# Two-layer perceiver kernel: the running maximum closed one tile earlier, and its scaling, the mask's bias and the decays rearranged on ScalarE

## The chip, the cores and the metric

The kernel runs on one core of one Trainium2 chip. The metric is the device time in microseconds (us) of one execution. The engines are TensorE (PE in the profile; its weight loads are PEld), VectorE (DVE), ScalarE (ACT), GpSimd (POOL) and SyncE (SP), whose queue issues the DMA transfers. Each engine works through its own instructions in order and waits on semaphores for the others.

## The reference, cut to what matters

128 latent rows of 256 numbers attend, in two layers, over the same context of 12,544 rows. Between the two attentions and behind the second lie small linear-attention, feed-forward and convolution blocks; the change does not touch their arithmetic.

```python
def _layer0_attention(q_in, ctx, mask, Wq, bq, Wk, bk, Wv, bv):    # 16 heads of 16
    q, k, v = split(q_in @ Wq.T + bq), split(ctx @ Wk.T + bk), split(ctx @ Wv.T + bv)
    scores = einsum('bhqd,bhkd->bhqk', q * 16 ** -0.5, k)
    scores = scores + ((1.0 - mask) * -10000.0)[:, None, :, :]     # first layer only
    probs = softmax(scores, axis=-1)
    return einsum('bhqk,bhkd->bhqd', probs, v)
...
x = x + _layer0_attention(layernorm(x), ctx, mask, ...)
x = x + linear_attention_block(layernorm(x)); x = x + ternary_ffn(layernorm(x))
x = x + _layer1_attention(layernorm(x), ctx, ctx, ...)             # no mask
x = x + rwkv_block(layernorm(x)); x = x + ternary_conv_ffn(layernorm(x))
```

The feed-forward weights are rounded to three values before use ("ternary").

## The kernel before, in words

The 12,544 context rows are 98 tiles of 128. Eight tiles are a group, so a layer has 13 groups: 12 full ones and one of two tiles. Groups are numbered through both layers: 0 to 12 are the first layer's (`m < NG`), 13 to 25 the second's. Tiles within a group are 0 to 7, so the "sixth tile" is number 5.

The softmax is computed online. For each group the kernel needs the running maximum of the scores per query and head before the group's scores are made. These maxima come from cheap bf16 products of queries and keys (`product`, L1396 on TensorE), 32 per full group, which VectorE reads one by one from PSUM (`maximum`, L989 with the mask added in the first layer, L992 in the second), into `tile_max`. The products and readings for the next group, and the first ones for the group after it, are spread over the tiles of the present group by `count_at`: four products in an ordinary tile. When the 32 are read, `chain` closes the group on VectorE: a reduction of `tile_max` (L1009), in the first layer a scaling and a shift (L1012), then a maximum with the group before (L1017), with a wait between each. It runs in tile 6 (`CHAIN_AT`). In tile 7 (`ROWS_AT`) TensorE turns the result (`turn_max`, L1490), ScalarE copies it out as `max_rows` (`rows_out`, L714) and GpSimd subtracts the rows of the group before (`max_change`, L586). In tile 0 of the next group ScalarE makes the decay factors by three exponentials (`decay_out`, L707: one of 128x256, two of 64x256) and VectorE multiplies the accumulated sums in PSUM by them (`decay_sums`, L1040), before TensorE may add that group's first sums (`weigh`, L1471).

One tile of the first layer goes as follows. TensorE makes the scores of 16 heads (L1446 subtracts the maximum, L1450 multiplies). VectorE adds the mask to half of them (`bias_first`, L1057). ScalarE copies the other half out (`copy_second`, L724), and GpSimd adds the mask there (`add_bias`, L580). ScalarE then takes the exponential of the first half (L732), copies a projection out (`keys_out` L691 in even tiles, `values_out` L699 in odd ones), and takes the exponential of the second half. TensorE meanwhile weighs the values of the tile before (L1471) and projects keys (L1389) or values (L1374) of groups to come. In the second layer there is no mask: ScalarE takes the exponential straight from PSUM (`exp_scores`, L738).

The mask of the next group is turned into a bias by two VectorE instructions of 128x512, in tiles 4 and 5 (`mask_bias`, L1066). In tile 2 of group 3 VectorE also adds a bias to x and scales a bias of the second layer (L1139, L1141, `BIAS_AT`). GpSimd rounds three feed-forward weights (`ternary`, L560, L562, L564) in 72 pieces, one in every tile of groups 1 to 9; `TERN_AT` says where.

From tile 2 of a layer's last full group on, the tiles are "lone" (`lone`, `LONE_FROM`): there are no more maxima, and in the first layer VectorE adds the mask to both halves (`bias_last`, L1075). In the first layer's lone tiles `weigh` also writes a small matmul into the `ps_proj` bank between its two halves, for which it first waits until the bank's last reader is through (`proj_free`). The two-tile group's maximum is closed in tile 2 and its rows are copied out in tile 7. GpSimd makes that last group's mask bias itself (`bias`, L548), in tile 4 of the group before. Behind the 72 pieces the SP queue loads the weights of the middle blocks (L508, L424), because they overwrite the place of the unrounded ones.

In the second layer, groups 13 and 14 are split into two halves with a maximum of their own each (`is_split`, `stage`).

Of the kernel before, what the change touches and what calls it, by code (L numbers as in the profile page):

```python
# [5 lines left out]
ALU = mybir.AluOpType  # L6
# [32 lines left out]
def perceiver(nc, a, out):  # L39

    with ExitStack() as ctx:
# [28 lines left out]
        tile_max = sb("tile_max", [P, H, 2])  # L70
        block_max = sb("block_max", [P, H])
# [75 lines left out]
        TERN_AT = tuple(range(GT))  # L147
# [11 lines left out]
        def run_max(m):  # L159
            return max_of_head[m % 2][:, :]  # L160
# [62 lines left out]
        def chained(m, t):  # L223
# [46 lines left out]
        CHAIN_AT, ROWS_AT = 6, 7  # L270
        FIRST_AHEAD = 2

        def count_at(m, t):
# [9 lines left out]
            elif m == 0:  # L283
                now = (2, 2, 2) if 0 < t < 3 else (2, 0, 2) if t < CHAIN_AT else (2, 0, 0) if t == CHAIN_AT else now
            elif n + 1 < NG and size(m + 1) < GT:
                now = ((2, 0, 2), (2, 0, 2), (2, 0, 0))[t] if t < 3 else now
            elif n + 1 < NG and t <= CHAIN_AT:
                now = (2, 0, 2 if t < CHAIN_AT else 0)
            if n + 2 < NG and m != NG:
                ahead = (0, 0, 2) if t == CHAIN_AT else (2, 0, 2) if t > CHAIN_AT else ahead  # L290
# [60 lines left out]
        BIAS_AT = 3  # L351
# [170 lines left out]
        def _(pool):  # L522
# [73 lines left out]
            for m in range(BLOCKS):  # L596
# [3 lines left out]
                for t in range(size(m)):  # L600
# [4 lines left out]
                    if 0 < m <= 9 and t in TERN_AT:  # L605
                        ternary(GT * (m - 1) + TERN_AT.index(t))
# [4 lines left out]
                    if rowed(m, t):  # L611
                        max_change(rowed(m, t))
                    if TAPS_AT <= m < TAPS_AT + FC // 2 and t in (1, 3, 5):
# [32 lines left out]
        def _(act):  # L646
# [55 lines left out]
            def decay_out(s):  # L702
                act.wait_ge(sig("max_changes"), decays(s))
                need("acc_decayed", decays(s) - 1)
                for to, of, cols in ((slice(0, P), slice(0, P), slice(0, D)), (slice(0, 64), slice(64, P), slice(D, 2 * D)),
                                     (slice(64, P), slice(0, 64), slice(D, 2 * D))):
# [33 lines left out]
            def lent_out(m, t):  # L740
                if decayed_in(m, t):
                    decay_out(stage(m, t))
                if rowed(m, t):
                    rows_out(rowed(m, t), turn_bank(m, t))

# [11 lines left out]
            for l in range(2):  # L757
# [14 lines left out]
                if l == 0:  # L772
# [7 lines left out]
                    for u in range(4, len(FIRST) - 1):  # L780
                        first_out(u)
                        if u in (7, 8):
                            abs_sum(u - 7)
# [1050 lines left out]
```

## Time and profile before

| What | us |
|---|---|
| Median of 3 runs (1011.79 to 1016.0) | 1012.31 |
| The profiled execution, its own time | 1009.68 |
| Span of that execution in the trace | 1008.0 |
| TensorE busy | 938.2 (93%) |
| VectorE busy | 737.4 (73%) |
| ScalarE busy | 684.1 (68%) |
| GpSimd busy | 407.5 (40%) |

Shares are over the whole span. The first layer's attention runs from about 40 to 484 us, the middle blocks to about 540, the second layer's attention to about 966, and the last blocks to the end. The profiled execution lies 2.6 us below the median; its span leaves out 1.7 us around it. A busy interval of a matmul in the trace is longer than the time that it holds the array, so intervals overlap and TensorE's idle time looks smaller than it is: the distance from a tile to the same point of the next one says more.

### The profile page before, as it was taken

What the parts mean: (1) busy time and instruction counts of PE and PEld (TensorE: products, weight loads), DVE (VectorE), ACT (ScalarE), POOL (GpSimd) and SP (SyncE); (2) the same over time, 40 slices, a digit from 0 to 9 for tenths busy, and PEclk for the clock granted to TensorE, in tenths of its full rate; (3) what the DMA queues carried; (4) which work ended last, traced back from release to release, by engine and by line L of the source; (5) the groups of instructions that cost most, each with busy time, mean ns of one, the idle gap of its engine ahead of it and who ended that gap; (6) DMA issues with size and microseconds to landing.
All of it is one profiled execution on the core that took longest, in us unless ns stands there. A gap on an engine that the chain in (4) does not pass through costs nothing.

```text
span 1008.0 us, 37248 instructions
## 1 busy us (share of the span) xinstructions
PE 938.2 (93%) x16290; PEld 575.7 (57%) x16291; DVE 737.4 (73%) x1594; ACT 684.1 (68%) x953; POOL 407.5 (40%) x365
## 2 busy tenths in 40 slices
PE   8899999999999999997887789999999999999877
PEld 3355555555555655555563455656656666566666
DVE  5798999999999899885447766556555666556566
ACT  2678878888887888876563456566666666665753
POOL 4258988899889988750100010011101001110010
PEclk9999999999999999999999899999999999999999
DMA  8402201211220210123005001011001101000000
GB/s 336 146 21 84 86 24 64 86 36 53 86 84 5 86 55 8 65 96 125 1 12 198 1 2 45 2 44 45 20 26 45 44 3 44 13 3 3 3 1 6
DMA packets 14994, 53.08 MB, mean 53 GB/s; under 512 B 4336, under 2 KB 5744, under 8 KB 10992
## 3 DMA queue, kind: packets, MB, share of 16 engines
q1 hardware_dynamic: 14832, 50.70, 14.4%
q8 instruction: 129, 2.11, 0.9%
q14 instruction: 33, 0.27, 0.1%
HBM read 50.56 MB, written 0.13 MB: 50 GB/s over the span
## 4 chain that ended last, share of the span: by engine, by line
PE 64%; DVE 16%; issue 12%; ACT 6%; DMA 1%; SPq 0%; DVEq 0%; ACTq 0%; POOLq 0%
PE ps_proj L1374 14%; PE ps_out L1471 13%; PE ps_scores L1450 11%; PE ps_proj L1389 8%; PE ps_max L1396 7%; DVE unread L989 4%; PE ps_scores L1446 3%; DVE tile_max L992 2%; ACT probs L738 2%; ACT decay L707 2%; DVE probs L1057 1%; DVE probs L1075 1%; DVE masks L1066 1%; DVE tile_max L989 1%; DVE ps_out L1040 1%
## 5 line engine op out<-in xcount | busy, mean ns | idle before, releaser
L992 DVE TENSOR_REDUCE tile_max<-ps_max 128x1 f32<-128x512 f32 (+1 forms) x293 | 188.3, 674 | 124.6 <-PE ps_max L1396 122.0
L580 POOL TENSOR_TENSOR probs<-probs,masks 128x512 f32<-128x512 f32 x180 | 227.5, 1286 | 69.4 <-ACT probs L724 68.8
L732 ACT ACTIVATE probs<-probs 128x1024 f32<-128x1024 f32 x196 | 207.0, 1056 | 71.6 <-DVE probs L1057 56.4
L738 ACT ACTIVATE probs<-ps_scores 128x1024 f32<-128x1024 f32 x192 | 186.3, 1021 | 86.2 <-PE ps_scores L1450 86.1
L1450 PE MATMUL ps_scores<-q_pad,k_full 32*128 32x256 f32 x3072 | 236.0, 376 | 0.0
L1471 PE MATMUL ps_out<-probs,values 128*32 128x128 f32 x6272 | 216.6, 277 | 4.8 <-DVE ps_out L1040 2.8
L989 DVE CUSTOM_DVE_ANT_0 unread<-ps_max,masks 128x512 bf16<-128x512 f32 (+1 forms) x293 | 189.8, 674 | 34.9 <-PE ps_max L1396 33.4
L1450 PEld LDWEIGHTS ps_scores<-q_pad,k_full 32*128 32x128 f32 x3072 | 189.1, 186 | 8.5
L1471 PEld LDWEIGHTS ps_out<-probs,values 128*32 128x32 f32 x6272 | 159.2, 110 | 57.6 <-issue 51.4
L1396 PE MATMUL ps_max<-k_high,q_high 32*128 32x512 bf16 (+1 forms) x590 | 155.9, 382 | 32.4 <-DVE tile_max L992 15.4
L1374 PE MATMUL ps_proj<-wv,ctx_t 128*32 128x256 f32 x2752 | 164.9, 380 | 0.0
L1389 PE MATMUL ps_proj<-ctx_t,wk 128*32 128x512 f32 (+1 forms) x1360 | 159.3, 586 | 1.0 <-DVE tile_max L989 0.8
L571 POOL CAST k_high<-k_full 128x1024 bf16<-128x1024 f32 (+1 forms) x51 | 50.3, 990 | 218.5 <-ACT k_full L691 141.7
L1396 PEld LDWEIGHTS ps_max<-k_high,q_high 32*128 32x128 bf16 x590 | 37.7, 91 | 173.8 <-issue 68.9
L586 POOL TENSOR_TENSOR max_step<-max_rows 128x512 f32<-128x512 bf16 x26 | 30.6, 1177 | 259.7 <-ACT max_rows L714 259.7
L1446 PE MATMUL ps_scores<-max_rows,minus 32*128 32x512 bf16 x768 | 110.2, 382 | 7.7 <-ACT max_rows L714 4.1
L1374 PEld LDWEIGHTS ps_proj<-wv,ctx_t 128*32 128x32 f32 x2752 | 82.3, 110 | 48.6 <-issue 0.5
L1057 DVE TENSOR_TENSOR probs<-ps_scores,masks 128x1024 f32<-128x1024 f32 x90 | 109.7, 1219 | 0.0
L724 ACT COPY probs<-ps_scores 128x512 f32<-128x512 f32 x180 | 95.6, 584 | 0.9 <-PE ps_scores L1450 0.9
L699 ACT COPY values<-ps_proj 128x512 f32<-128x512 f32 x86 | 50.0, 582 | 47.6 <-PE ps_proj L1374 47.1
L691 ACT ACTIVATE k_full<-ps_proj,bk 128x512 f32<-128x512 f32 (+1 forms) x85 | 56.8, 669 | 29.7 <-PE ps_proj L1389 29.4
L1396 PE MATMUL ps_proj<-k_high,q_high 32*128 32x512 bf16 (+1 forms) x182 | 67.8, 372 | 2.1 <-ACT k_full L691 2.1
(302 smaller groups left out, 858.7 us busy)
## 6 DMA issues: line engine op xcount, KB each, us to landing
ctx_t<-in_ctx_t SPq DMA_DIRECT2D x23, 1024.0 KB, 5.9
masks<-in_mask_n SPq DMA_DIRECT2D x12, 512.0 KB, 3.6
masks<-in_mask_t SPq DMA_DIRECT2D x12, 512.0 KB, 4.0
room_w<-in_L_attn_f_w SPq DMA_DIRECT2D x2, 1024.0 KB, 9.0
room_w<-in_L_ffn_w SPq DMA_DIRECT2D x2, 1024.0 KB, 7.4
ctx_t<-in_ctx_t SPq DMA_DIRECT2D x2, 512.0 KB, 6.5
room_w<-in_L_ffn_w_gate SPq DMA_DIRECT2D x1, 1024.0 KB, 11.4
room_w<-in_L_ffn_w_up SPq DMA_DIRECT2D x1, 1024.0 KB, 13.8
```

The costliest lines, as they stand in the source:

```text
L580: nc.gpsimd.tensor_tensor(p, p, three(mask_t[m % 2], GT)[:, t, :].unsqueeze(1).to_broadcast([P, 4, P]), ALU.add).then_inc(sig("bias_added" ...
L732: nc.scalar.activation(prob(T, half), prob(T, half), ACT.Exp).then_inc(sig(f"exp_done{half}"), 1)
L738: nc.scalar.activation(prob(T, half), scores_in(m, t, half).rearrange("p a n -> p (a n)"), ACT.Exp).then_inc(sig(f"exp_done{half}"), 1)
L989: ins = v.tensor_tensor_reduce(unread[:, j % 2, 0:width(m)], max_bank(m, j)[:, 0:width(m)], mask_n[m % 2][:, half_cols(m, half)], 1.0, -3e ...
L992: ins = v.tensor_reduce(tile_max[:, h, half:half + 1], max_bank(m, j)[:, 0:width(m)], AX_X, ALU.max)
L1057: v.tensor_tensor(prob(T, 0).rearrange("p (h q) -> p h q", h=8), ps_scores[:, 0:2, :].rearrange("p a (h q) -> p (a h) q", q=P), three(mask ...
L1374: last = mm(bank[32 * g:32 * (g + 1), D * (t - at.start):D * (t - at.start + 1)], ctx_t[m % 3][:, t, c, keys], wv[l][:, c, :], start=(c == ...
L1389: last = mm(bank[32 * g:32 * (g + 1), 0:width(m)], wk[l][:, c, dims], ctx_t[m % 3][:, 4 * half:min(4 * half + 4, size(m)), c, :], start=(c ...
L1396: mm(bank[:, 0:width(m)], q_high[rows, c, zz, :], k_high[m % 2][rows, c, half_cols(m, half)], start=True, stop=True).then_inc(sig("max_rea ...
L1446: mm(banks[g], minus16[rows, :], max_rows[stage(m, t) % 2][rows, :], start=True, stop=True)
L1450: last = mm(banks[g][:, D * c:D * (c + 1)], k_full[m % 3][rows, c, P * t:P * (t + 1)], q_pad[rows, c, :], start=False, stop=True, skip_gro ...
L1471: last = mm(ps_out[VW * g:VW * (g + 1), P * c:P * (c + 1)], values[m % 2][:, t, h, :], prob(T, half)[:, P * o:P * (o + 1)], start=(t == 0 ...
```

## The change

1. The first layer's full groups close the next group's maximum in tile 5 in place of 6, and copy its rows out in tile 6 in place of 7 (`chain_at`, `rows_at`); `count_at` moves the readings to fit: of the 32 maxima of a group, the first ten (before: six) are now read right behind the closing of the group ahead of it. Group 0 gets six maxima in its tiles 3 and 4. The two-tile group is closed in tile 1 (first layer) or 2 (second), and in both layers its rows are copied out in tile 3.
2. `tile_max` has four columns, the running maximum being column 0 or 3 by turns, so that one reduction gives the new running maximum. Scaling, shift and conversion to bf16 become one ScalarE instruction on 128x16 (`max_out`), in both layers (a plain copy in the second), for which `turn_max` waits.
3. The mask's bias of groups 1 to 11 goes from VectorE to ScalarE (`mask_bias`), ahead of the first exponential of tiles 4 and 5.
4. The decays: in the first layer's full groups the 128x256 one is made in tile 7 and the other two in tile 0. They stand ahead of the tile's exponentials, in the second layer too, where all three stay in the first tile of a stage.
5. GpSimd's ternary pieces go to tiles 1, 2, 4, 5 and 7 of groups 1 to 10, five in group 0, and 17 in tiles 2 and 3 of group 11, behind that tile's `max_change`. The addition and scaling of `BIAS_AT` go from group 3, tile 2, to group 11, tile 4.

```diff
-        TERN_AT = tuple(range(GT))
+        TERN_AT = [(0, t) for t in range(3, 8)] + [(m, t) for m in range(1, 11) for t in (1, 2, 4, 5, 7)] + [(11, 2)] * 9 + [(11, 3)] * 8
...
-            return max_of_head[m % 2][:, :]
+            return tile_max[:, :, (3, 0)[m % 2]:(3, 0)[m % 2] + 1]
...
-            return stage(m + 1) if t == (CHAIN_AT if size(m + 1) == GT else LONE_FROM) else None
+            return stage(m + 1) if t == (chain_at(m) if size(m + 1) == GT else LONE_FROM - (m < NG)) else None
...
-            return stage(m, SPLIT) if is_split(m) and t == SPLIT - 1 else stage(m + 1) if t == ROWS_AT and m % NG + 1 < NG else None
+            return stage(m + 1) if t == (rows_at(m) if size(m + 1) == GT else LONE_FROM + 1) else None
...
-        CHAIN_AT, ROWS_AT = 6, 7
+        def chain_at(m):
+            return 5 if m < NG else 6
+        def rows_at(m):
+            return chain_at(m) + 1
...
-        BIAS_AT = 3
+        BIAS_AT = NG - 2
...
+            def max_out(s):
+                act.wait_ge(sig("max_chain"), s + 1)
+                need("max_turned", s - 1)
+                if s < NG:
+                    nc.scalar.activation(max_of_head[s % 2][:, :], run_max(s).rearrange("p h o -> p (h o)"), ACT.Identity,
+                                         scale=1 / MASK_SCALE, bias=mask_shift).then_inc(sig("max_set"), 1)
...
+            def mask_bias(m, part):
...
+                nc.scalar.activation(t, t, ACT.Identity, scale=1 / MASK_SCALE, bias=mask_shift).then_inc(sig("bias_t"), 1)
...
+            def decays_out(m, t):
+                early = m + 1 < NG and size(m + 1) == GT and t == size(m) - 1
+                if early:
+                    decay_out(stage(m + 1), 0)
+                if decayed_in(m, t):
+                    if m >= NG or size(m) < GT:
+                        decay_out(stage(m, t), 0)
+                    decay_out(stage(m, t), 1)
...
                         elif l == 0:
                             copy_second(T)
...
+                            decays_out(m, t)
                             lent_out(m, t)
+                            if m + 2 < NG and t in (4, 5):
+                                mask_bias(m + 1, t - 4)
                             exp_in_place(m, t, 0)
+                            chained_out(m, t)
                             projected(m, t)
                             exp_in_place(m, t, 1)
                         else:
+                            decays_out(m, t)
                             exp_scores(m, t, int(lone(m, t)))
...
-                ins = v.tensor_reduce(block_max[:, :], tile_max[:, :, 0:1] if one else tile_max[:, :, :], AX_X, ALU.max)
-                if m < NG:
-                    link(ins)
-                    ins = v.scalar_tensor_tensor(out=block_max[:, :], in0=block_max[:, :], scalar=1 / MASK_SCALE,
-                                                 in1=mask_shift.to_broadcast([P, H]), op0=ALU.mult, op1=ALU.add)
-                ins.then_inc(c, 1)
-                dve.wait_ge(c, 2 * m + 1)
-                need("max_turned", m - 1)
-                v.tensor_tensor(run_max(m), block_max[:, :], run_max(m - 1), ALU.max).then_inc(c, 1)
-                dve.wait_ge(c, 2 * m + 2)
+                cols = (slice(0, 2) if one else slice(0, 3), slice(1, 4, 2) if one else slice(1, 4))[s % 2]
+                v.tensor_reduce(run_max(s), tile_max[:, :, cols], AX_X, ALU.max).then_inc(sig("max_chain"), 1)
+                dve.wait_ge(sig("max_chain"), s + 1)
...
-            def mask_bias(m, part):
-                b = m % 2
-                dve.wait_ge(sig(f"mask_t_loaded{b}"), m // 2 * 16 + 16)
-                t = mask_t[b][:, half_cols(m, part)]
-                v.scalar_tensor_tensor(out=t, in0=t, scalar=10000.0, in1=mask_shift.to_broadcast([P, HALF]),
-                                       op0=ALU.mult, op1=ALU.add).then_inc(sig("bias_t"), 1)
...
-                pe.wait_ge(sig("max_chain"), 2 * m + 2)
+                pe.wait_ge(sig("max_set"), m + 1)
```

## Rows read from the trace of the kernel before

**Rows 1.** Busy time by engine (windows), tile 0 of group 1 to tile 0 of group 10:
```profile
81.39:407.52 326.13, 316.89 (x5912) 189.51 (x5908) 299.50 (x705) 271.20 (x397) 289.31 (x244) 1.00 0.17 57
```
**Rows 2.** Timeline of VectorE, group 4 and start of group 5: start, duration, instruction, [idle before]:
```profile
203.64 1.22 DVE L1057 TENSOR_TENSOR probs<-ps_scores,masks 128x1024 f32<-128x1024 f32 x1
...
206.06 0.69 DVE L989 CUSTOM_DVE_ANT_0 unread<-ps_max,masks 128x512 bf16<-128x512 f32 x1 [0.60 <-PE ps_max L1396]
...
207.90 1.22 DVE L1057 TENSOR_TENSOR probs<-ps_scores,masks 128x1024 f32<-128x1024 f32 x1
...
209.64 1.79 DVE L1066 SCALAR_TENSOR_TENSOR masks<-masks,small 128x512 f32<-128x512 f32 x1
...
213.19 1.21 DVE L1057 TENSOR_TENSOR probs<-ps_scores,masks 128x1024 f32<-128x1024 f32 x1
...
214.93 0.68 DVE L1066 SCALAR_TENSOR_TENSOR masks<-masks,small 128x512 f32<-128x512 f32 x1
...
217.45 1.22 DVE L1057 TENSOR_TENSOR probs<-ps_scores,masks 128x1024 f32<-128x1024 f32 x1
...
219.31 0.19 DVE L1009 TENSOR_REDUCE block_max<-tile_max 128x16 f32<-128x32 f32 x1
219.53 0.51 DVE L1012 SCALAR_TENSOR_TENSOR block_max<-block_max,small 128x16 f32<-128x16 f32 x1
...
222.45 1.22 DVE L1057 TENSOR_TENSOR probs<-ps_scores,masks 128x1024 f32<-128x1024 f32 x1
...
226.91 1.22 DVE L1057 TENSOR_TENSOR probs<-ps_scores,masks 128x1024 f32<-128x1024 f32 x1
...
235.72 1.22 DVE L1057 TENSOR_TENSOR probs<-ps_scores,masks 128x1024 f32<-128x1024 f32 x1
```
**Rows 3.** Timeline of ScalarE, an ordinary tile of group 4 and tile 0 of group 5:
```profile
204.89 1.06 ACT L732 ACTIVATE probs<-probs 128x1024 f32<-128x1024 f32 x1 [0.71 <-DVE probs L1057]
...
227.18 1.32 ACT L707 ACTIVATE decay<-max_step 128x256 f32<-128x256 f32 x3
```
**Rows 4.** Groups of instructions by line, whole span: count, busy us, mean ns, idle before:
```profile
L691 ACT ACTIVATE k_full<-ps_proj,bk 128x512 f32<-128x512 f32 (+1 forms) x85 | 56.8, 669 | 29.7 <-PE ps_proj L1389 29.4
...
L560 POOL TENSOR_SCALAR room_w<-room_w,small 128x256 f32<-128x256 f32 x24 | 30.1, 1254 | 0.0
```
**Rows 5.** Timeline of VectorE, group 0, a tile with six maxima:
```profile
47.39 1.22 DVE L1057 TENSOR_TENSOR probs<-ps_scores,masks 128x1024 f32<-128x1024 f32 x1
...
52.93 1.22 DVE L1057 TENSOR_TENSOR probs<-ps_scores,masks 128x1024 f32<-128x1024 f32 x1
```
**Rows 6.** Timeline of TensorE, the first layer's last tiles:
```profile
473.55 0.39 PE L1446 MATMUL ps_scores<-max_rows,minus 32*128 32x512 bf16 x4 [2.73 <-ACT max_rows L714]
...
480.47 0.64 PE L1471 MATMUL ps_out<-probs,values 128*32 128x128 f32 x16 [2.83 <-DVE ps_out L1040]
```
**Rows 7.** Timeline of GpSimd, group 11, behind its last mask addition:
```profile
449.80 1.08 POOL L548 TENSOR_SCALAR masks<-masks 128x256 f32<-128x256 f32 x1
```
**Rows 8.** Timeline of the SP queue and its DMA issues (KB, us to landing), 446 to 472 us:
```profile
453.73 1.25 SPq L424 DMA_DIRECT2D room_w<-in_L_attn_f_b  x1
...
room_w<-in_L_attn_f_b SPq DMA_DIRECT2D x1, 128.0 KB, 10.0
```
**Rows 9.** Timeline of VectorE, second layer, tile 0 of group 16:
```profile
659.00 1.29 DVE L992 TENSOR_REDUCE tile_max<-ps_max 128x1 f32<-128x512 f32 x2 [1.96 <-PE ps_max L1396]
...
663.25 0.70 DVE L1040 TENSOR_TENSOR ps_out<-ps_out,decay 128x512 f32<-128x512 f32 x1 [1.77 <-ACT decay L707]
663.86 1.28 DVE L992 TENSOR_REDUCE tile_max<-ps_max 128x1 f32<-128x512 f32 x2
```
**Rows 10.** Timeline of ScalarE in the same tile:
```profile
660.10 1.94 ACT L738 ACTIVATE probs<-ps_scores 128x1024 f32<-128x1024 f32 x2 [0.80 <-PE ps_scores L1450]
```
**Rows 11.** Timeline of TensorE, second layer, a split stage and the last group:
```profile
567.96 1.20 PE L1396 MATMUL ps_max<-k_high,q_high 32*128 32x512 bf16 x2 [2.99 <-DVE tile_max L992]
...
959.38 0.39 PE L1446 MATMUL ps_scores<-max_rows,minus 32*128 32x512 bf16 x4 [1.33 <-ACT max_rows L714]
```

More of the change, by code:

```diff
@@ L283, in count_at @@
             elif m == 0:
-                now = (2, 2, 2) if 0 < t < 3 else (2, 0, 2) if t < CHAIN_AT else (2, 0, 0) if t == CHAIN_AT else now
+                now = (2, 2, 2) if 0 < t < chain_at(m) else (2, 0, 2) if t == 0 else (2, 0, 0) if t == chain_at(m) else now
             elif n + 1 < NG and size(m + 1) < GT:
-                now = ((2, 0, 2), (2, 0, 2), (2, 0, 0))[t] if t < 3 else now
-            elif n + 1 < NG and t <= CHAIN_AT:
-                now = (2, 0, 2 if t < CHAIN_AT else 0)
+                now = ((2, 0, 2), (2, 0, 2), (2, 0, 0))[t + (m < NG)] if t + (m < NG) < 3 else now
+            elif n + 1 < NG and t <= chain_at(m):
+                now = (2, 0, 2 if t < chain_at(m) else 0)
             if n + 2 < NG and m != NG:
-                ahead = (0, 0, 2) if t == CHAIN_AT else (2, 0, 2) if t > CHAIN_AT else ahead
+                ahead = (0, 0, 2) if t == chain_at(m) else (2, 0, 2) if t > chain_at(m) else ahead
             return own, now, ahead
@@ L612, in _ @@
                         max_change(rowed(m, t))
+                    for i in range(len(TERN_AT)):
+                        if TERN_AT[i] == (m, t):
+                            ternary(i)
                     if TAPS_AT <= m < TAPS_AT + FC // 2 and t in (1, 3, 5):
@@ L700, in values_out, with decay_out @@
                                bank[:, 0:D * (at.stop - at.start)].rearrange("p (t h d) -> p t h d", h=H, d=HD)).then_inc(sig("v_copied"), 1)
[L702 to L706, printed above, removed]
+            def max_out(s):
[4 more added lines that the diff above has]
+                                         scale=1 / MASK_SCALE, bias=mask_shift).then_inc(sig("max_set"), 1)
+                else:
+                    nc.scalar.copy(max_of_head[s % 2][:, :], run_max(s).rearrange("p h o -> p (h o)")).then_inc(sig("max_set"), 1)
+            def mask_bias(m, part):
+                b = m % 2
+                act.wait_ge(sig(f"mask_t_loaded{b}"), m // 2 * 16 + 16)
+                t = mask_t[b][:, half_cols(m, part)]
+                nc.scalar.activation(t, t, ACT.Identity, scale=1 / MASK_SCALE, bias=mask_shift).then_inc(sig("bias_t"), 1)
+            def decay_out(s, part):
+                if part == 0:
+                    act.wait_ge(sig("max_changes"), decays(s))
+                    need("acc_decayed", decays(s) - 1)
+                    pieces = [(slice(0, P), slice(0, P), slice(0, D))]
+                else:
+                    pieces = [(slice(0, 64), slice(64, P), slice(D, 2 * D)), (slice(64, P), slice(0, 64), slice(D, 2 * D))]
+                for to, of, cols in pieces:
                     nc.scalar.activation(decay[to, cols], max_step[of, cols], ACT.Exp).then_inc(sig("decay_ready"), 1)
@@ L783, in _ @@
                             abs_sum(u - 7)
+                max_out(NG * l)
                 rows_out(NG * l)
@@ L1153, in _ @@
                             chain(chained(m, t))
-                        if m + 2 < NG and t in (4, 5):
-                            mask_bias(m + 1, t - 4)
                         for k, j in ahead:
```

36 lines of the change are left out of this document (21 added, 15 removed).

## The prediction, made before the change was timed

> **What bounds the kernel now.** I read the busy time by stretch first, then VectorE's timeline of whole groups, ScalarE's beside it, and TensorE's waits at the ends of groups and layers. In groups 1 to 9 of the first layer [rows 1] TensorE is busy 316.89 of 326.13 us and VectorE 299.50, so either could be the bound; the 9.2 us that TensorE seems idle understate what can be won, since its intervals overlap.
>
> The distance from one mask addition (L1057) to the next is the tile's pitch [rows 2]. An ordinary tile takes 207.90 - 203.64 = 4.26, and VectorE idles 0.60 in it, waiting for a product: TensorE sets this pitch. Longer ones in the same group:
> - tile 4: 213.19 - 207.90 = 5.29, +1.03; the first mask half (L1066) takes 1.79 there.
> - tile 5: 4.26, although the second half (0.68) sits in it: what VectorE does at that place is free up to the 0.60.
> - tile 6: 222.45 - 217.45 = 5.00, +0.74: three dependent steps from 219.31 on.
> - tile 7: 226.91 - 222.45 = 4.46, +0.20 (TensorE turns the maximum).
> - tiles 0 and 1 of the next: 235.72 - 226.91 = 8.81, +0.29: VectorE's multiplication of the sums, 0.70 [rows 9] in the free 0.60, is about 0.08 of it, and ScalarE, held by 1.32 us of decays in tile 0 [rows 3], the other 0.21.
>
> Together 2.26. Nine groups take 326.13 [rows 1], 36.24 each, against 8 x 4.26 = 34.08; my group gives 34.08 + 2.26 = 36.34, so it stands for the rest.
>
> In the second layer VectorE has time, but at tile 0 it waits 1.77 for the decays, and from 659.00 to 663.86 it is 4.86 [rows 9]: 0.60 over 4.26. Ends of layers and stages have waits of 1.3 to 3.0 us [rows 6, 11].
>
> **Part by part: ordinary groups of the first layer.** VectorE loses both mask halves; the 1.03 of tile 4 goes. ScalarE takes them, ahead of an exponential for which it idles 0.71 (the smaller of the two kinds of tile) [rows 3]. No row shows this instruction. Nearest is L691, also 128x512 with a bias, 0.67 [rows 4]; starts behind one another come about 0.1 before the end of the one before, so it holds the engine 0.57 and fits. Upper bound: GpSimd's bias of half that size took 1.08 [rows 7], so 2.16; at the lower bound, nothing, the sum is the same, since the gap hides it anyway. I take 0.67: cost 0. Without the gap it would be 0.57 twice a group.
>
> The closing becomes one reduction, 0.19, and its wait, some 0.3 in the free 0.60: the 0.74 goes. Its bounds are 0.19 and the 0.51 of the neighbouring L1012 [rows 2]; both fit. The Trainium skill (GPSIMD Engine Reference, § Specifications) says that VectorE and GpSimd contend when a VectorE instruction reads two SBUF operands; by that, L1066 and L1012 are slow for this reason and the new reduction, with one operand, stays at 0.19; the sum is the same by either.
>
> ScalarE gets `max_out`, 128x16, behind the first exponential of tile 5. What queues behind it are the projection's copy and the second exponential, for which TensorE's second half of `weigh` waits almost at once. No such instruction stands in the trace; between 0 and the 0.41 a piece of L707 took (1.32 / 3 [rows 3]) less overlap, I take 0.15 a group.
>
> The decays are split: one (0.4) in tile 7's gap, two (0.9) in tile 0's, where 1.32 stood. What overran is gone or is 0.1, so the 0.21 goes. Turn (0.20) and VectorE's multiplication (0.08) stay. GpSimd has 8 x 2.5 of additions, 5 pieces and three other ops, under 30 us in 34.5, and is no bound. New group: 34.08 + 0.20 + 0.08 + 0.15 = 34.5. Nine groups: 326.13 - 310.5 = **-15.6** (the x bias of group 3 is in it; lone tiles have room for it).
>
> **Group 0.** Tiles 3 and 4 have six maxima. Such a tile takes 52.93 - 47.39 = 5.54 [rows 5]: +1.28 over 4.26 in tile 3, about +0.6 in tile 4, which loses its mask half; tiles 5 to 7 give back 0.5. **+1.4**; bounds 0 and 2.5.
>
> **Group 10** was shorter already (fewer projections), so about two thirds of a group's 1.74: **-1.2**; bounds 0 and -1.74.
>
> **End of the first layer.** Four fewer products and no closing in lone tiles: -0.7. Rows of group 12, copied out in tile 3, end TensorE's 2.73 [rows 6] all but 0.1: -2.6. Decays ahead of the exponentials let VectorE multiply right behind its mask additions, so of 2.83 [rows 6] some 2.3 go. Against it: in lone tiles the small matmul into `ps_proj` must now wait for that copy, behind two exponentials: +1.0. **-4.6**.
>
> The queues behind it: GpSimd is through its additions at 449.8 [rows 7] and now has 17 pieces there. At the mean 1.25 [rows 4] they take 21.3, with `max_change` and the bias of group 12 some 2.3 more: 473.4, where VectorE wants that bias at about 472 (the place of the first row of [rows 6], less what is saved before it). Pieces without contention are nearer 1.1, so 0 to 1.5 late; I take 0. The SP queue then loads the middle weights: the last issue ended at 454.98 and landed 10.0 later, 465 [rows 8], 15.2 behind the point at which GpSimd was through. From 470 this gives 485, where the middle block wants them at about 485 (ten us behind the second row of [rows 6], less what the end of the layer saves). I take 0, bound +3.
>
> **Second layer.** At tile 0 the decays, some 1.3, now run in ScalarE's wait for scores, 0.80 [rows 10]; the exponentials come about 0.5 later and end near 662.5, before the next scores, whose readers start at 663.86 [rows 9] at the earliest. The 1.77 goes, and the 0.60 with it: nine full groups, **-5.4**; three more such places (tiles 0 of groups 14 and 24, tile 4 of 14) at the same 0.60, **-1.8**. At the split of group 13 TensorE waited 2.99 [rows 11]; VectorE can start 1.6 earlier: **-1.6**. In the last group the rows come early: -1.3 of 1.33 [rows 11] and some 0.5 of the decay wait behind it: **-1.8**. `max_out` is off the path except at the layer's start (0.1).
>
> **Sum:** -15.6 + 1.4 - 1.2 - 4.6 - 5.4 - 1.8 - 1.6 - 1.8 = -30.6. The profiled execution would go from 1009.68 to 979.1. The median of the runs lies 2.6 above it, so 1012.31 - 30.6 = 981.7, **982 us**.
>
> **Rivals.**
> - *ScalarE gives out in the first layer.* It is busy 271 of 326 us [rows 1] and gets about 1.4 us a group. For it: the gap is 0.71 and the load 0.57, and every second exponential is awaited. If a mask half takes 1.3 (twice L691), it overruns by 1.3 - 0.1 - 0.71 = 0.5 at 22 places: 11 us given back, 993.
> - *The second layer's decays buy nothing,* since the exponentials behind them come 0.5 late and TensorE waits instead. Against it: they would still end near 662.5. Price: 5.4 + 1.8 + 1.6 + 1.8 = 10.6 back: 992.
> - *More than I count:* the products' waits shrink beside the mask halves, group 0 costs nothing, the decay waits go whole. 1.4 + 2 + 3: 975.
> - *Slower.* The mask halves hold ScalarE, and with it TensorE, for longer than VectorE's excess was. At the bound of 2.16 each overruns by 1.35, 22 x 1.35 = 29.7: about 1011, no change. To be 5 us slower each must hold ScalarE for (30.6 + 5) / 22 + 0.81 = 2.4 us: then 1017 or more. Nothing near it stands in ScalarE's rows.
>
> **How the numbers follow.** Forecast (976 to 988) 0.62; ScalarE gives out 0.12; second layer buys nothing 0.12; more than counted 0.07; no change, the first rival's far end, 0.03; slower 0.04. About 0.5%, 5 us, is what a measurement of this kernel can tell from no change. Faster 0.93, same 0.03, slower 0.04. The range takes the forecast's own, the gain beyond it, and the two partial failures to their values: 975 to 994. It leaves out some 0.15.
>
> **What would show it.** In the new profile: pitches of 4.26 in tiles 4 to 6 of the first layer but for one of 4.46, a group of 34.5; L1066 and L1012 gone; the new ScalarE instruction of 128x512 near 0.67 and its exponential still waiting for VectorE; rows of [rows 6] at 0.4; tile 0 in the second layer at 4.26. Wrong would be: a group over 35.2, TensorE waiting for L732 in tile 5 or 6, VectorE waiting for GpSimd's L548, TensorE waiting for a DMA behind the first layer.

## The result: 979.8 us, where 982 was predicted

| | us |
|---|---|
| Before, median of 4 runs (1010.85 to 1016.0) | 1012.05 |
| After, median of 4 runs (976.58 to 979.94) | 979.8 |
| Ratio, 95% interval | 0.9667 (0.9634 to 0.9700) |
| Profiled executions, before and after | 1009.68 and 976.58 |

The change makes the kernel 3.3% faster. The prediction was 982, range 975 to 994, built on a profiled execution that goes from 1009.68 to 979.1.

The profile after, in the views that answer to the rows of before. Busy time by engine (windows), from tile 0 of group 1 to tile 0 of group 10:

```profile
81.26:391.86 310.60, 310.60 (x5916) 190.08 (x5908) 271.01 (x669) 282.50 (x425) 253.85 (x216) 1.00 0.18 60
```

The nine groups of [rows 1] went from 326.13 to 310.60 us: -15.53. Behind the window's length stand the busy times of TensorE, its weight loads, VectorE, ScalarE and GpSimd, then the granted clock and the DMA's share and GB/s. TensorE, which seemed idle for 9.2 us, now shows no idle time; VectorE is 28.5 us less busy, ScalarE 11.3 more.

VectorE's timeline of group 4, as in [rows 2]:

```profile
184.91 1.22 DVE L1098 TENSOR_TENSOR probs<-ps_scores,masks 128x1024 f32<-128x1024 f32 x1
...
197.71 1.22 DVE L1098 TENSOR_TENSOR probs<-ps_scores,masks 128x1024 f32<-128x1024 f32 x1
...
201.97 1.22 DVE L1098 TENSOR_TENSOR probs<-ps_scores,masks 128x1024 f32<-128x1024 f32 x1
...
206.23 1.22 DVE L1098 TENSOR_TENSOR probs<-ps_scores,masks 128x1024 f32<-128x1024 f32 x1
208.09 0.20 DVE L1058 TENSOR_REDUCE tile_max<-tile_max 128x16 f32<-128x48 f32 x1
208.85 0.69 DVE L1037 CUSTOM_DVE_ANT_0 unread<-ps_max,masks 128x512 bf16<-128x512 f32 x1 [0.56 <-PE ps_max L1428]
210.69 1.22 DVE L1098 TENSOR_TENSOR probs<-ps_scores,masks 128x1024 f32<-128x1024 f32 x1
215.14 1.22 DVE L1098 TENSOR_TENSOR probs<-ps_scores,masks 128x1024 f32<-128x1024 f32 x1
219.40 1.22 DVE L1098 TENSOR_TENSOR probs<-ps_scores,masks 128x1024 f32<-128x1024 f32 x1
```

The first row is tile 0, then tiles 3, 4, 5, 6, 7 and the next group's tile 0. Tile 4 (201.97 to 206.23) takes 4.26 where it took 5.29. Tile 5, which closes the maximum, takes 4.46, and tile 6, in which TensorE turns it, 4.45. The group takes 219.40 - 184.91 = 34.49.

ScalarE's timeline of tiles 4, 5 and 7 of that group and of the next tile 0 [rows 3]:

```profile
202.31 0.73 ACT L725 ACTIVATE masks<-masks,small 128x512 f32<-128x512 f32 x1
203.23 1.06 ACT L760 ACTIVATE probs<-probs 128x1024 f32<-128x1024 f32 x1 [0.19 <-DVE probs L1098]
...
206.65 0.74 ACT L725 ACTIVATE masks<-masks,small 128x512 f32<-128x512 f32 x1
207.48 1.06 ACT L760 ACTIVATE probs<-probs 128x1024 f32<-128x1024 f32 x1
208.44 0.30 ACT L716 ACTIVATE max_of_head<-tile_max,small 128x16 bf16<-128x16 f32 x1
...
215.48 0.44 ACT L735 ACTIVATE decay<-max_step 128x256 f32<-128x256 f32 x1
216.39 1.06 ACT L760 ACTIVATE probs<-probs 128x1024 f32<-128x1024 f32 x1 [0.47 <-DVE probs L1098]
...
219.86 0.85 ACT L735 ACTIVATE decay<-max_step 64x256 f32<-64x256 f32 x2
```

The mask half takes 0.73, 0.06 more than the estimate, and in tile 4 the exponential behind it still waits 0.19 for VectorE: it fits the gap. In tile 5 the gap is just used up: the exponential starts 0.09 behind the half's end (206.65 + 0.74 = 207.39).

TensorE's waits at the end of the first layer [rows 6], then in the second layer's split and last group [rows 11]:

```profile
441.43 0.30 PE L1508 MATMUL ps_proj<-ident 128*32 128x128 f32 x1 [0.76 <-ACT max_rows L742]
454.36 0.40 PE L1478 MATMUL ps_scores<-max_rows,minus 32*128 32x512 bf16 x4 [0.35 <-DVE probs L1109]
458.87 0.65 PE L1503 MATMUL ps_out<-probs,values 128*32 128x128 f32 x16 [0.43 <-DVE ps_out L1081]
...
544.66 0.39 PE L1428 MATMUL ps_max<-k_high,q_high 32*128 32x512 bf16 x1 [1.23 <-DVE tile_max L1040]
...
929.45 0.39 PE L1478 MATMUL ps_max<-max_rows,minus 32*128 32x512 bf16 x2 [0.87 <-ACT probs L766]
```

At the place of the 2.73 for the rows (454.36, the last group's first scores) TensorE now waits 0.35, for VectorE, and the 2.83 for the decayed sums is 0.43. The new wait for the `ps_proj` bank stands at 441.43, with 0.76. In the second layer the split's 2.99 is 1.23, and the last group's 1.33, for the rows, is 0.87, for ScalarE's exponentials.

GpSimd's groups of instructions in 430:452 (busy us, mean ns, idle before) [rows 4]:

```profile
L571 POOL TENSOR_SCALAR room_w<-room_w 128x256 f32<-128x256 f32 x8 | 8.3, 1064 | 0.0
L573 POOL TENSOR_SCALAR tern<-room_w 128x256 bf16<-128x256 f32 x8 | 6.7, 866 | 0.0
```

The timeline of GpSimd and of the SP queue, its bias for group 12 and the last issue of the middle weights, then that transfer [rows 7, 8]:

```profile
449.86 1.07 POOL L557 TENSOR_SCALAR masks<-masks 128x256 f32<-128x256 f32 x1
...
455.01 0.61 SPq L433 DMA_DIRECT2D room_w<-in_L_attn_f_b  x1
```
```profile
room_w<-in_L_attn_f_b SPq DMA_DIRECT2D x1, 128.0 KB, 7.7
```

The 17 pieces take 0.87 to 1.14 each and end at 449.8. VectorE wants the bias at 455.81, and the weights have landed at 455.0 + 7.7 = 462.7, before the middle block starts at 469.17. Neither is late.

VectorE in the second layer, tile 0 of group 16 [rows 9], and ScalarE in it [rows 10]:

```profile
632.92 1.29 DVE L1040 TENSOR_REDUCE tile_max<-ps_max 128x1 f32<-128x512 f32 x2 [1.96 <-PE ps_max L1428]
...
635.32 0.69 DVE L1081 TENSOR_TENSOR ps_out<-ps_out,decay 128x512 f32<-128x512 f32 x1
...
637.14 1.29 DVE L1040 TENSOR_REDUCE tile_max<-ps_max 128x1 f32<-128x512 f32 x2 [1.13 <-PE ps_max L1428]
```
```profile
633.15 1.29 ACT L735 ACTIVATE decay<-max_step 128x256 f32<-128x256 f32 x3
634.48 1.94 ACT L766 ACTIVATE probs<-ps_scores 128x1024 f32<-128x1024 f32 x2
```

From reading to reading it is 637.14 - 632.92 = 4.22 where it was 4.86: the decays run while ScalarE would have waited for scores.

The whole, by stretches of the two traces:

| Stretch | before | after | change | predicted |
|---|---|---|---|---|
| start to the first mask addition | 41.16 | 39.81 | -1.35 | 0 |
| group 0 | 40.23 | 41.45 | +1.22 | +1.4 |
| groups 1 to 9 | 326.13 | 310.60 | -15.53 | -15.6 |
| group 10 | 34.54 | 33.24 | -1.30 | -1.2 |
| end of the first layer (to the division of its sums) | 44.64 | 40.00 | -4.64 | -4.6 |
| middle blocks | 59.04 | 59.11 | +0.07 | 0 |
| second layer | 423.23 | 411.54 | -11.69 | -10.6 |
| rest | 39.03 | 39.15 | +0.12 | 0 |
| span | 1008.0 | 974.9 | -33.1 | -30.6 |

The -1.35 at the start is not the change's: the load of `bq` landed 1.07 earlier in this execution. The same kernel, profiled again, reached that point at 40.63, its variants between 39.91 and 40.99.

### The profile page after: what moved, and what is told of

Same layout as the page of the kernel before. It is cut to its first block, busy times and chain, and to the rows that moved or that the text cites. A ratio compares the mean times of both kernels' runs of the same rounds, so it can differ in the third digit from the quotient of the medians.

```text
span 974.9 us, 37261 instructions
## 1 busy us (share of the span) xinstructions
PE 928.5 (95%) x16290; PEld 575.1 (59%) x16291; DVE 701.2 (72%) x1531; ACT 701.1 (72%) x1003; POOL 398.6 (41%) x365
## 4 chain that ended last, share of the span: by engine, by line
PE 53%; issue 32%; DVE 7%; ACT 4%; POOL 3%; DMA 1%; SPq 0%; DVEq 0%; POOLq 0%; ACTq 0%
PE ps_out L1503 11%; PE ps_scores L1482 9%; PE ps_proj L1406 9%; PE ps_proj L1421 8%; PE ps_max L1428 5%; PE ps_scores L1478 2%; POOL k_high L580 2%; DVE tile_max L1040 1%; ACT probs L766 1%; PE ps_scores L1421 1%; DVE probs L1109 1%; POOL tern L628 1%; DMA bq<-in_L_xattn_bq 1%; ACT probs L760 1%; DVE unread L1037 1%
## 5 line engine op out<-in xcount | busy, mean ns | idle before, releaser
L1421 PEld LDWEIGHTS ps_proj<-ctx_t,wk 128*32 128x32 f32 x1360 | 36.6, 109 | 57.3 <-issue 48.6
```

What stands on the lines that cost most here:

```text
L1421: last = mm(bank[32 * g:32 * (g + 1), 0:width(m)], wk[l][:, c, dims], ctx_t[m % 3][:, 4 * half:min(4 * half + 4, size(m)), c, :], start=(c ...
```

## Experiments

The unit is again the distance between mask additions. Groups 1 to 9 take 310.60 in the changed kernel; the rows are group 2's unless said otherwise. Behind each time stand the ratio to the kernel before, measured beside it, and its 95% interval.

**Mask halves back on VectorE.**

```diff
-                            if m + 2 < NG and t in (4, 5):
-                                mask_bias(m + 1, t - 4)        # ScalarE
...
                             chain(chained(m, t))
+                        if m + 2 < NG and t in (4, 5):
+                            mask_bias(m + 1, t - 4)            # VectorE
```

> The changed kernel with one part undone: the mask's two halves go back to VectorE, behind the closing in tiles 4 and 5 of groups 0 to 10. Theory (VectorE has 0.60 us free in a tile and the halves overran it): tile 4 goes from 4.26 to about 5.3, and tile 5, which now holds the closing too, from 4.46 to about 4.8; 1.3 us a group, a full group of 35.8, and 980 + 11 x 1.3 = 994. Rival (ScalarE, relieved of 2 x 0.64 us a group, gives half of it back): 987. Rival (what was slow was the closing, not the halves): 981.

988.15 (0.9761, 0.973 to 0.9791); the nine groups take 318.08, a group 35.34: tile 4 4.86, tile 5 4.73. So +0.83 a group, less than the 1.3 expected. The time lies near the first rival's 987, but ScalarE's relief is not needed to explain it: the first half is shorter than the 1.79 it was expected from. VectorE's two instructions in group 2, and what GpSimd did then:

```profile
136.93 1.36 DVE L1105 SCALAR_TENSOR_TENSOR masks<-masks,small 128x512 f32<-128x512 f32 x1
142.14 0.88 DVE L1105 SCALAR_TENSOR_TENSOR masks<-masks,small 128x512 f32<-128x512 f32 x1
```
```profile
135.22 2.52 POOL L589 TENSOR_TENSOR probs<-probs,masks 128x512 f32<-128x512 f32 x2 [0.66 <-ACT probs L752]
137.71 1.50 POOL L571 TENSOR_SCALAR room_w<-room_w 128x256 f32<-128x256 f32 x1
...
142.07 1.06 POOL L571 TENSOR_SCALAR room_w<-room_w 128x256 f32<-128x256 f32 x1
```

Begun inside GpSimd's additions (135.22 to 137.74), the instruction takes 1.36; begun behind them, beside a piece, 0.88. The piece that starts while the 1.36 runs takes 1.50, the one beside the 0.88 takes 1.06. In the kernel before, the same instruction had cost 1.79 in the group that the prediction read, and 0.68 to 1.81 over all 22. GpSimd's additions in that group, beside the two halves of [rows 2]:

```profile
208.37 2.51 POOL L580 TENSOR_TENSOR probs<-probs,masks 128x512 f32<-128x512 f32 x2
...
212.53 2.53 POOL L580 TENSOR_TENSOR probs<-probs,masks 128x512 f32<-128x512 f32 x2
```

The half that began at 209.64 ran until 0.55 behind the end of the addition (210.88 - 209.64 = 1.24, and 1.79 - 1.24 = 0.55). The one at 214.93 began 0.13 before such an end and took 0.68. All 22 halves of the kernel before fit this: what was left of GpSimd's addition of 128x512, plus 0.54 to 0.56. So do ten of the eleven first halves here; the eleventh met no addition and took 0.69. It is as if VectorE's instruction made no progress until the addition inside which it begins is over. Group 4's tile 4 stood 1.03 over 4.26, the mean of nine groups 0.89. The total by group rested on the mean, so the sum did not suffer. The Trainium skill (GPSIMD Engine Reference, § Specifications) says that the two engines contend when VectorE reads two SBUF operands; the traces agree, and the closing's reduction, which reads one, takes 0.19 to 0.21 in the changed kernel although 12 of its 13 begin inside such an addition.

**ScalarE makes each half twice.** The added one writes into a buffer that nobody reads.

```diff
+                nc.scalar.activation(spare_b[:, :], t, ACT.Identity, scale=1 / MASK_SCALE, bias=mask_shift)...
                 nc.scalar.activation(t, t, ACT.Identity, scale=1 / MASK_SCALE, bias=mask_shift)...
```

> The changed kernel, but ScalarE makes each half of the mask's bias twice, the first time into a buffer that nobody reads: 22 more instructions of 128x512, 0.64 us each. It measures ScalarE's room in tiles 4 and 5. Prediction's theory (a gap of 0.71 us and 0.1 of slack, of which one half takes 0.6): a second one overruns by about 0.5, 22 x 0.5 = 11, so 991, with pitches near 4.75 in tiles 4 and 5. Rival (ScalarE has more room than the gap shows, since what waits for its exponentials has slack of its own): under 2 us in all, 980 to 982. Rival (no room at all was left): 22 x 0.64 = 14, 994.

986.9 (0.9742, 0.9709 to 0.9775), between the theory and the rival with more room; a group 35.09: tile 4 4.29, tile 5 4.77, tile 6 4.69. Two more instructions, which hold ScalarE for 0.63 each, cost 0.59 together. In tile 4 the second one was almost free, in tiles 5 and 6 it was not:

```profile
135.83 0.73 ACT L728 ACTIVATE spare_b<-masks,small 128x512 f32<-128x512 f32 x1
136.46 0.72 ACT L729 ACTIVATE masks<-masks,small 128x512 f32<-128x512 f32 x1
137.07 1.05 ACT L764 ACTIVATE probs<-probs 128x1024 f32<-128x1024 f32 x1
```

The exponential no longer waits for VectorE. By this, ScalarE's room in tile 4 was the 0.19 shown above and, as an estimate (0.63 less 0.19 less the 0.03 that the tile grew), about 0.4 of slack behind its exponentials. The second half's lateness carries through the closing tile into the next. So the rival "ScalarE gives out" was real at twice the load, and cost 6 us by the first layer's stretches, not the 11 it was priced at. Another 3.35 of this trace lies in the second layer, which the edit does not touch, where the clock was 0.68 over 528:544.

**Three steps on VectorE**, closing still in tile 5; ScalarE's `max_out` goes in the first layer.

```diff
                 v.tensor_reduce(run_max(s), ...).then_inc(sig("max_chain"), 1)
+                if s < NG:
+                    link(v.scalar_tensor_tensor(out=block_max[:, :], in0=run_max(s)..., scalar=1 / MASK_SCALE,
+                                                in1=mask_shift.to_broadcast([P, H]), op0=ALU.mult, op1=ALU.add))
+                    v.tensor_copy(max_of_head[s % 2][:, :], block_max[:, :]).then_inc(sig("max_set"), 1)
```

> The changed kernel, still closing in tile 5, but in the first layer VectorE scales, shifts and converts the running maximum itself (reduction, then the two-operand step, then a copy to bf16, each waiting for the one before) and ScalarE has no max_out there. Theory (the old closing cost a tile about 0.7 us through its chain of dependent steps, the new one costs 0.20 through ScalarE): tile 5 goes from 4.46 to about 4.95, a group from 34.49 to about 35.0, 980 + 11 x 0.5 = 985.5. Rival (the steps hid in VectorE's free 0.60 and what cost was their meeting with GpSimd's pieces, which now lie elsewhere): tile 5 at 4.3 to 4.5, 978 to 981.

982.16 (0.9714, 0.97 to 0.9729), between theory and rival; tile 5 4.81, a group 34.83: +0.34 (34.88 in the mean of nine).

```profile
141.60 0.20 DVE L1061 TENSOR_REDUCE tile_max<-tile_max 128x16 f32<-128x48 f32 x1
141.84 0.60 DVE L1064 SCALAR_TENSOR_TENSOR block_max<-tile_max,small 128x16 f32<-128x16 f32 x1
142.48 0.33 DVE L1067 CAST max_of_head<-block_max 128x16 bf16<-128x16 f32 x1
142.72 0.68 DVE L1040 CUSTOM_DVE_ANT_0 unread<-ps_max,masks 128x512 bf16<-128x512 f32 x1
```

The reading behind follows at once, so VectorE sets this tile. The 0.60 again begins inside one of GpSimd's additions and ends just behind it; the same instruction took 0.18 where it met none.

**The title's edit undone**: closing in tile 6, rows in tile 7, all three decays in tile 0 (ahead of its exponentials).

```diff
         def chain_at(m):
-            return 5 if m < NG else 6
+            return 6
...
-                early = m + 1 < NG and size(m + 1) == GT and t == size(m) - 1
+                early = False
```

> The changed kernel with the title's edit undone: first-layer groups close the next maximum in tile 6 and copy its rows out in tile 7, group 0 and the readings as before, the two-tile group closed in tile 2; since the rows come later, all three decays stand in tile 0, ahead of its exponentials. Theory (the earlier closing buys nothing in itself): group 0 gives back 1.2, the end of the layer costs 0.7 more, tile 0 of ten groups some 0.2 more: 980 + 1.5 = 981.5, between 979 and 983. Rival (the early closing and the split decays that it makes possible carry a good part of the gain): a group of 35 or more, 986 or more.

979.9 (0.9668, 0.9643 to 0.9693), the same as the changed kernel within what can be told. Its stretches show two sides that nearly cancel: a group takes 34.76 in the mean (+0.25, in tiles 0 and 1, 4.34 + 4.47 against 4.26 + 4.28, while the 0.20 of tile 5 moves to tile 7; +2.2 for the nine), group 10 +0.27, the end of the layer +0.65; group 0, without the stretch of low clock in its tile 1 (see below), gives back 2.0. Net +1.1 us by the trace. In tile 0 ScalarE's exponential follows its three decays without a wait for VectorE, so ScalarE holds that tile; late rows and unsplit decays go together here and were not told apart.

**The scaling moved on ScalarE.**

```diff
                             exp_in_place(m, t, 0)
-                            chained_out(m, t)
                             projected(m, t)
                             exp_in_place(m, t, 1)
+                            chained_out(m, t)
```

> The changed kernel with one instruction moved: ScalarE scales the closed maximum (128x16) behind the second exponential of tile 5, not ahead of the projection's copy and of that exponential. Theory (the 0.20 us of tile 5 is that instruction on the path of the second exponential): tile 5 goes back to 4.26, 11 x 0.20 = 2.2 less, 977.6. Rival (it then holds up the next tile's copy out of PSUM, or the turning of the maximum on TensorE, by the same time): 979.8, with tile 6 longer by what tile 5 loses.

978.22 (0.9672, 0.9657 to 0.9686), tile 5 still 4.46, a group 34.49. Both accounts fall: neither tile 5 nor tile 6 moved. The 0.20 of the closing tile is not ScalarE's. Group 2 of the changed kernel's trace shows where it is: TensorE begins the product for VectorE 2.00 behind the mask addition in tile 4 (134.99 - 132.99) and in tile 5 (139.25 - 137.25) alike, but VectorE takes it up 2.42 behind it in tile 4 and 2.62 in tile 5.

**VectorE's waits around the closing.** First the order of two waits, then their number.

```diff
-                dve.wait_ge(sig("max_ready"), J + 1)
                 if m < NG and j == 0:
                     dve.wait_ge(sig(f"mask_n_loaded{m % 2}"), m // 2 * 16 + 16)
+                dve.wait_ge(sig("max_ready"), J + 1)
```

> The changed kernel with one wait of VectorE moved: ahead of the first reading of the group after next, which stands right behind the closing, it waits for that group's mask before it waits for TensorE's product, not after it. Theory (the 0.20 us of the closing tile, which stayed when the scaling was moved on ScalarE, is VectorE taking up that reading 0.23 late, behind a product that ended at 139.64 in group 2, because further waits stand behind the one for the product): tile 5 goes from 4.46 to 4.26, a group to 34.3, 11 x 0.2 = 2.2 less, about 977.6. Rival (the lateness comes from the closing's own wait or from TensorE): group at 34.49, 979.8.

978.97 (0.9662, 0.9637 to 0.9686); tile 5 4.50. The order is not the cause.

```diff
-                if j == 0:
+                if j == 0 and not 1 < m < NG:
                     need("max_chain", stage(m))
...
-                    if j == 0:
+                    if j == 0 and m < 2:
                         dve.wait_ge(sig(f"mask_n_loaded{m % 2}"), ...)
...
+                        if m + 2 < NG and t == chain_at(m):      # at the start of the closing tile
+                            dve.wait_ge(sig(f"mask_n_loaded{m % 2}"), (m + 2) // 2 * 16 + 16)
```

> The changed kernel with two of VectorE's waits taken out from between the closing and the reading behind it: the wait for the mask of the group after next moves to the start of the closing tile, and a second wait for the closing, which repeats one just passed, goes. Order alone did not help (moving the mask's wait ahead of the product's left tile 5 at 4.50), so the theory now is that each wait that stands by itself costs VectorE some 0.1 us even when it is met: 0.56 us lie between the reduction's end and the reading, the product is there after 0.33, and two waits fewer leave about 0.36. Tile 5 goes to 4.26 to 4.30, a group to 34.3, about 978. Rival (the time is in the closing's own wait, or on TensorE): a group at 34.49, 979.8.

979.33 (0.968, 0.966 to 0.9701). VectorE's reading behind the closing:

```profile
140.98 0.20 DVE L1058 TENSOR_REDUCE tile_max<-tile_max 128x16 f32<-128x48 f32 x1
141.64 0.69 DVE L1037 CUSTOM_DVE_ANT_0 unread<-ps_max,masks 128x512 bf16<-128x512 f32 x1 [0.46 <-PE ps_max L1430]
```

The idle time fell from 0.56 to 0.46 with two waits fewer, and tile 5 from 4.46 to 4.36; the wait that was put ahead of the mask addition lengthened tile 4 from 4.26 to 4.32. So a wait that is already met costs VectorE 0.05 to 0.06, by these two differences, and half of the 0.20 was such waits. What the other 0.10 is stays open.

**GpSimd's pieces back in every tile** of groups 1 to 9.

```diff
+        TERN_AT = [(m, t) for m in range(1, 10) for t in range(8)]
```

> The changed kernel with GpSimd's 72 pieces back where they were, one in every tile of groups 1 to 9 and none behind. Theory (GpSimd has slack in every tile, and VectorE has no instruction left that is slowed by it): a group of 34.5, the end of the layer the same, 980. Rival (in tiles 0, 3 and 6 GpSimd has a copy or the subtraction of the rows as well, 2.5 + 1.1 + 1.1 us against a pitch of 4.26, so that its additions come late there): about 0.3 in each of three tiles, a group of 35.4, 988.

979.38 (0.9662, 0.9638 to 0.9687). A group takes 34.65 in the mean, +0.14, most of it in tile 5: the new places are worth 1.3 us, nearer to nothing than to the rival's 8.

**Decays behind the exponentials** in the second layer and in the first's last group.

```diff
-                            decays_out(m, t)
                             exp_scores(m, t, int(lone(m, t)))
                             exp_scores(m, t, 1 - int(lone(m, t)))
+                            decays_out(m, t)
```

> The changed kernel with the decays put back behind the tile's two exponentials in the second layer and in the first layer's last group. Theory: tile 0 of each full group of the second layer goes back from 4.22 to 4.85 with VectorE waiting 1.8 us for the decays (nine groups, 5.7 us), the other stages give back 0.6 each and the split of group 13 about 1.7 (3.5 us together), the last groups of the two layers about 2.3 and 0.5: 980 + 12 = 992. Rival (the gain came from the new way of closing and from the rows copied out early, and the decays only followed): 981 to 983.

996.06 (0.9833, 0.9802 to 0.9863), 16 to 18 over the changed kernel. The period of the second layer's groups is 34.75 again, and all the old waits are back:

```profile
462.77 1.08 PE L1503 MATMUL ps_out<-probs,values 128*32 128x128 f32 x16 [2.83 <-DVE ps_out L1081]
```

They give +2.4 at the end of the first layer and about +12 in the second. The other 7 us of this trace lie where stretches at a lower clock stand: about 1.4 in group 0, 2.5 at the end of the first layer, 1.5 in the second layer and 1.4 behind it. Three of these stretches, busy time (windows) with the granted clock third from the right:

```profile
44.00:52.00 8.00, 6.90 (x103) 3.95 (x107) 4.79 (x14) 5.68 (x9) 2.50 (x2) 0.79 0.68 131
460.00:472.00 12.00, 8.50 (x80) 5.85 (x81) 4.23 (x9) 6.08 (x9) 0.00 (x0) 0.72 0.18 60
552.00:564.00 12.00, 8.77 (x114) 6.04 (x114) 7.97 (x14) 5.00 (x8) 0.00 (x0) 0.72 0.01 1
```

**The same edit alone, in the kernel before.**

```diff
-                if decayed_in(m, t):
+                if decayed_in(m, t) and m < NG:          # behind the exponentials
                     decay_out(stage(m, t))
...
+                            if decayed_in(m, t):
+                                decay_out(stage(m, t))
                             exp_scores(m, t, int(lone(m, t)))
```

> The kernel before with one part of the change alone: in the second layer the three decays stand ahead of the tile's exponentials. Theory: tile 0 of its full groups goes from 4.85 to 4.22 (nine groups, 5.7 us) and the split groups give 3 to 4 more, the last group nothing, since its rows come late: 1011 - 9 = 1002, the first layer unchanged at 36.24 us a group. Rival (without the other parts the exponentials that start later hold TensorE up): 1009 to 1011.

1002.71 against 1011.6 (0.9914, 0.989 to 0.9938): -8.9. The first layer is unchanged (326.20 for the nine groups), the second goes from 423.23 to 414.85. This part works without the others up to the last two groups: those take 29.20 (from the first exponential of group 24 to that of the last tile), 0.96 more than before, and 25.87 in the changed kernel. There it needs the early rows, as the next run shows.

**Rows late**: the two-tile group's rows in tile 7 in place of 3.

```diff
-            return ... rows_at(m) if size(m + 1) == GT else LONE_FROM + 1 ...
+            return ... rows_at(m) if size(m + 1) == GT else GT - 1 ...
```

> The changed kernel, but the rows of the two-tile group are copied out in tile 7 again, not in tile 3, in both layers. Prediction's account: TensorE waits 2.6 us more ahead of the first layer's last group and 1.3 more ahead of the second's, and the wait of 0.76 for the bank in the lone tiles goes: +3.1, and since the decays now stand ahead of that group's exponentials and need these rows, up to 1 more in each layer: 983 to 985. Rival (the decays behind the rows are what the ends hang on, and the rows buy nothing by themselves): 980 to 981.

983.82 (0.9732, 0.9716 to 0.9749). The end of the first layer takes 43.15, +3.15: the old 2.73 is back, the 0.76 is gone, and behind the wait the clock was 0.75 over 456:460 and 0.83 over 460:464. The second layer's last stretch takes 2.29 more. TensorE, then ScalarE behind it:

```profile
457.51 0.40 PE L1478 MATMUL ps_scores<-max_rows,minus 32*128 32x512 bf16 x4 [2.73 <-ACT max_rows L742]
...
936.13 0.39 PE L1478 MATMUL ps_max<-max_rows,minus 32*128 32x512 bf16 x2 [1.88 <-ACT probs L766]
```
```profile
458.72 1.29 ACT L735 ACTIVATE decay<-max_step 128x256 f32<-128x256 f32 x3 [1.27 <-POOL max_step L595]
...
933.64 1.29 ACT L735 ACTIVATE decay<-max_step 128x256 f32<-128x256 f32 x3 [1.72 <-POOL max_step L595]
```

Decays that stand first wait for GpSimd's difference of late rows (1.27 in the first layer, 1.72 in the second), and the exponentials wait behind them: in the second layer TensorE waits 1.88 for one where it waited 0.87. Early rows and decays ahead belong together.

**The changed kernel again**, beside the run with fewer waits.

> The changed kernel itself, once more, beside the run above on the same chip: 979.8, with groups of 34.49. Its start (39.81 us to the first mask addition in the first profile, 39.8 to 41.7 in the others) and tile 1 of group 0 (5.54 or 6.9 to 7.2) show what varies between executions of one kernel.

978.27 (0.9668, 0.9652 to 0.9683), groups of 34.49, start 40.63. Of the variants, 978.22, 978.97, 979.33 and 979.38 do not differ from it by more than the runs scatter: none beats it.

## Why the prediction was right, step by step

**Ordinary groups** (-15.6, measured -15.53). The reading that TensorE sets a pitch of 4.26 and that all above it can be removed held: undoing the parts one at a time gives +0.83 (mask halves), +0.34 (steps of the closing), +0.25 (closing early, with split decays) and +0.14 (pieces), 1.56 of the 1.73 that a group became shorter in the mean. Another 0.09 is the x bias, which made tile 2 of group 3 take 5.08. The mask half at 0.67 was 0.73 and hidden. `max_out` at 0.15 a group was the right size with the wrong cause: ScalarE's instruction costs nothing where it stands, and the closing tile's 0.20 is VectorE's, at least half of it waits that it passes. VectorE's multiplication at 0.08 was nothing: tiles 0 and 1 take 8.54 with it. So the 0.27 that the undone title shows there, with unsplit decays behind late rows, is not VectorE's, and the 0.21 given to the decays was a little small.

**Group 0** (+1.4, measured +1.22): the total is near, the terms are not, and this is luck. Tile 3 grew by 1.04 (predicted 1.28) and tiles 5 to 7 gave back 0.3 (0.5), but tile 4 became 0.14 shorter where 0.6 more was expected, and the missing 0.61 stands in tile 2 (6.46 for 5.85), which the prediction left out.

**Group 10** (-1.2, measured -1.30) and the **end of the first layer** (-4.6, -4.64) came as summed. At that end the rows' wait gave 2.38 for 2.6, the decays' 2.40 for 2.3, and the bank's wait was 0.76 for 1.0. The queues were taken as just not late. By the prediction's own terms the last piece would have ended at about 472 (473.4 less the bias's 1.08), not at the 470 from which it counted the weights. The slip did no harm, since the queues had room: 17 pieces took 16.1 us, not 21.3, since a piece takes 0.95 in the mean there, not 1.25, so GpSimd was through 4.9 us before VectorE asked.

**Second layer** (-10.6, measured -11.69). The full groups gave 0.63 for 0.60. The split groups gave 3.9 for 2.8 (in group 13, by TensorE's scores, tile 4 gave 1.75 and tile 5 0.8; the clock was low there in both traces, so the two cannot be held apart from it), group 24 with the last group 1.9 for 2.4. The decays alone are worth 8.4 there; rival two, that they buy nothing, was wrong by all of it.

**Title's edit.** The prediction had it pay through a shorter tile 0 and the end of the layer, less group 0's six readings: right, and the net is about 1.1 us. Nearly all of the gain is elsewhere.

The forecast of the median, 982, is 2.2 above 979.8 and 3.7 above the repeat. Of the 2.2, 1.1 is the second layer and 1.35 the shorter start of this execution; against it, the median lies 3.2 above the profiled execution in place of the 2.6 that was taken over.

## What to carry to other kernels

Measure the pitch of an undisturbed step and of each disturbed one: the excess is what can be won, and it names the engine; busy shares do not. An instruction moved to another engine is free only while its gap and the slack behind it last, which doubling it measures. An instruction moved ahead of others in a queue brings its own inputs' lateness with it: give those the same lead.

## What the runs showed of the hardware

The same two-operand VectorE instruction of 128x512 took from 0.68 to 1.81 us: 0.55 and what was left of the GpSimd addition inside which it began. Begun 0.05 to 0.07 behind the start of a one-operand GpSimd piece it took 0.87 to 0.95. GpSimd's piece that began inside it took 1.50 in place of 1.06. A wait already met costs VectorE about 0.05.

The granted clock fell to the lower of its two levels in some stretches and not in others of the same work. With the decays behind, 44:52 had 0.79 (above) and tile 1 of group 0 took 6.91 us; in the changed kernel the clock stayed at 1.00 and it took 5.54, both times it was profiled, though TensorE had waited 1.6 for a copy just ahead of it in both. Six of the other variants show the same fall and a tile of 6.9 to 7.2. Behind the wait that ended at 462.77 the clock was 0.72 over 460:472 (0.50 in 464:468, which is 1.2 GHz), and the layer's last sums took 2.5 longer: ScalarE waited 3.27 for them where it waited 0.76. In the kernel before, the same wait of 2.83 [rows 6] was followed by no fall, but its wait of 2.99 [rows 11] by 0.72 over 564:576. The changed kernel had 0.86 over 540:564. So part of what a wait costs can lie behind it, and this part differs between executions of the same work; a sum over waits leaves it out. What decides whether the clock falls, no run shows.
